# Running-sum copies of v's seven products on VectorE, new orders on every engine, and two small VectorE operations in another form

## The reference, cut to what matters

```python
x  = L0_attn_x                          # (16, 512, 256)
xn = layernorm(x)
q, k, v = xn @ wq, xn @ wk, xn @ wv     # 8 heads of 128
s  = rope(q) @ rope(k).T / 128          # causal mask, then softmax
attn = (softmax(s) @ v) @ wo
h  = relu(s0 * ([xn, -xn] @ sign(k0))) * 2
h  = relu(s1 * (h @ sign(k1))) * 2
ffn = s2 * (h @ sign(k2))
out = x + attn + ffn
```

## Time and profile before

| | |
|---|---|
| median of 3 runs | 1731.85 us |
| the profiled execution's own time | 1731.84 us |
| its span | 1730.0 us |
| TensorE matmuls busy | 1698.8 us, 98% |
| ScalarE busy | 1515.6 us, 88% |
| VectorE busy | 1429.8 us, 83% |
| GpSimd busy | 970.0 us, 56% |

### The profile page before, as it was taken

One profiled execution on the slowest core, in us unless ns is written; L12 is line 12 of the kernel. 1 busy time (PEld: TensorE's weight loads), 2 busy tenths in 40 slices (PEclk: granted clock), 3 DMA queues, 4 the chain that ended last, 5 costly groups with the idle time before them and its releaser, 6 DMA issues.

```text
span 1730.0 us, 35715 instructions
## 1 busy us (share of the span) xinstructions
PE 1698.8 (98%) x13340; PEld 1259.3 (73%) x13340; DVE 1429.8 (83%) x3440; ACT 1515.6 (88%) x3310; POOL 970.0 (56%) x775
## 2 busy tenths in 40 slices
PE   6999999999999999999999999999999999999998
PEld 3567767777777777777877777777777777777777
DVE  8997888787888888788787887878888887987875
ACT  6898898988989889898998989889898898989984
POOL 7764745557465474654656455474654746546441
PEclk9999999999999999999999999999999999999999
DMA  5243534434434454445344434344354445344343
GB/s 176 49 78 65 100 66 92 91 69 80 88 84 80 79 82 74 92 68 95 68 77 86 86 80 88 72 81 86 84 83 80 80 74 92 68 98 71 66 86 68
DMA packets 486046, 142.05 MB, mean 82 GB/s; under 512 B 465904, under 2 KB 484848, under 8 KB 485872
## 3 DMA queue, kind: packets, MB, share of 16 engines
q1 hardware_dynamic: 485872, 139.76, 42.6%
HBM read 14.94 MB, written 8.39 MB: 13 GB/s over the span
## 4 chain that ended last, share of the span: by engine, by line
PE 89%; DVE 3%; ACT 3%; DMA 3%; SPq 1%; issue 1%; POOL 0%; DVEq 0%
PE bank L276 33%; PE bank L806 21%; PE bank L774 11%; PE bank L757 11%; PE bank L795 8%; PE bank L817 5%; DMA pt<-ph 2%; DMA ph<-in_wv 1%; SPq L324 1%; DVE bank L663 1%; ACT ph L509 1%; ACT bank L505 1%; DVE ph L673 0%; DVE mx L670 0%; ACT tb L485 0%
## 5 line engine op out<-in xcount | busy, mean ns | idle before, releaser
L416 POOL TENSOR_TENSOR tb<-tb,sin 128x512 f32<-128x512 f32 x256 | 326.7, 1277 | 326.9 <-ACT tb L485 325.1
L419 POOL TENSOR_TENSOR qk<-tb,qk 128x512 f16<-128x512 f32 x256 | 298.1, 1167 | 286.2 <-ACT qk L488 285.5
L806 PE MATMUL bank<-hb,wa 128*128 128x256 f16 x3360 | 382.2, 273 | 0.0
L806 PEld LDWEIGHTS bank<-hb,wa 128*128 128x128 fp8e5 x3360 | 327.4, 98 | 43.3
L505 ACT ACTIVATE bank<-bank,nm,sc 128x512 f32<-128x512 f32 (+3 forms) x512 | 302.1, 590 | 3.4
L673 DVE SCALAR_TENSOR_TENSOR ph<-bank,mx,ph 128x512 f16<-128x512 f32 (+3 forms) x512 | 253.0, 543 | 16.3 <-ACT ph L509 15.7
L509 ACT ACTIVATE ph<-bank,mx 128x512 f16<-128x512 f32 (+3 forms) x512 | 232.5, 540 | 24.2 <-DVE mx L670 22.3
L663 DVE CUSTOM_DVE_ANT_0 bank<-bank,mask 128x512 f32<-128x512 f32 (+3 forms) x512 | 239.6, 512 | 13.0 <-PE bank L757 12.7
L774 PE MATMUL bank<-pt,v 128*128 128x256 f16 (+1 forms) x2304 | 232.5, 256 | 7.0 <-DMA pt<-ph 3.4
L757 PE MATMUL bank<-qk 128*128 128x512 f16 (+3 forms) x1536 | 230.0, 299 | 4.0 <-DVE tb L639 2.6
L774 PEld LDWEIGHTS bank<-pt,v 128*128 128x128 f16 x2304 | 203.5, 98 | 39.6 <-DMA pt<-ph 6.1
(11 more groups left out here) (138 smaller groups left out, 2617.4 us busy)
## 6 DMA issues: line engine op xcount, KB each, us to landing
out<-xnat SPq DMA_DIRECT2D x32, 256.0 KB, 2.1
xnat<-in_x SPq DMA_DIRECT2D x15, 512.0 KB, 3.9
pt<-ph SPq DMA_TRANSPOSE x256, 4.3
o<-in_k SPq DMA_DIRECT2D x1, 1024.0 KB, 8.3
v<-in_wq SPq DMA_DIRECT2D x1, 1024.0 KB, 10.4
v<-in_wk SPq DMA_DIRECT2D x1, 1024.0 KB, 12.0
ph<-in_wv SPq DMA_DIRECT2D x1, 1024.0 KB, 13.7
o<-in_wo SPq DMA_DIRECT2D x1, 1024.0 KB, 10.8
```

Source lines behind the costliest of these rows:

```text
L416: pool.tensor_tensor(tb, tb, SIN[:], ALU.mult).then_inc(s_crossed, 1)
L419: pool.tensor_tensor(QK[:, g % 2, 2 * w + 1, :], TB[:, (2 * g + w) % TRING, :], QK[:, g % 2, 2 * w, :], ALU.subtract).then_inc(s_qk_lo, 1)
L806: mm = pe.matmul(ps[:, 256 * u:256 * u + 256], WA[:, w, k, (2 * j + u) * 128:(2 * j + u) * 128 + 128], HB[:, h, s, k, :], start=first and ...
```

## The change

- The two copies of v's running sums per group are made by `copy_v` on VectorE and counted by a semaphore of their own, `s_vcopy`; the second layer's copies stay on ScalarE.
- The written orders of all five queues are laid anew, with other banks, other places of the loop's cut, and other waits; the set of operations is otherwise the same.
- The last instruction of `power_of_two` is split into two of one column each.
- The multiplication in `inverse` goes over its four columns in the order 0, 2, 1, 3, as a pattern of two by two with steps 1 and 2.

```diff
+        s_vcopy = sem("s_vcopy")
...
-            dve.tensor_scalar(DG[:, i:i + 2], ID[:, 0:2], AR[:, i + 1:i + 2], 2.0 ** -6,
+            dve.tensor_scalar(DG[:, i:i + 1], ID[:, 0:1], AR[:, i + 1:i + 2], 2.0 ** -6, ALU.mult, ALU.mult)
+            dve.tensor_scalar(DG[:, i + 1:i + 2], ID[:, 1:2], AR[:, i + 1:i + 2], 2.0 ** -6,
                               ALU.mult, ALU.mult).then_inc(s_pow, 1)
...
+        def every_other(v):
+            return v.rearrange("p (a b) -> p b a", a=2)
+
         def inverse(dve, g):
             dve.reciprocal(RI[:, g % 4, :], SM[:, g % 4, :]).then_inc(s_recip, 1)
             dve.wait_ge(s_recip, g + 1)
-            dve.tensor_scalar(RK[:, g % 4, :], RI[:, g % 4, :], 4096.0, None, ALU.mult).then_inc(s_inv, 1)
+            dve.tensor_scalar(every_other(RK[:, g % 4, :]), every_other(RI[:, g % 4, :]), 4096.0, None,
+                              ALU.mult).then_inc(s_inv, 1)
```

SyncE, batch 2 (the transposes of heads 21 and 22 change places; the loop has the same exchange in every batch):

```diff
-            sp.wait_ge(s_P_lo, 88)
+            sp.wait_ge(s_P_lo, 92)
             sp.wait_ge(s_PV, 20)
+            turn_p(sp, 22)
+            sp.wait_ge(s_PV, 21)
             turn_p(sp, 21)
-            sp.wait_ge(s_P_lo, 92)
-            sp.wait_ge(s_PV, 21)
-            turn_p(sp, 22)
```

The second group's copies of v in the loop, TensorE and VectorE after the change (these lines are all new):

```diff
+                scores(pe, 8 * b, 2, ps[4])
+                pe.wait_ge(s_P_lo, 32 * b - 3)
+                qk(pe, 8 * b + 1, 0, ps[2])
+                pe.wait_ge(s_P_lo, 32 * b - 1)
+                layer2(pe, 1, ps[6])
+                pe.wait_ge(s_P_lo, 32 * b)
+                v_product(pe, b, 1, 1, ps[0])
+                pe.wait_ge(s_o, 8 * b - 2)
+                qk(pe, 8 * b + 2, 0, ps[5])
+                pe.wait_ge(s_vcopy, 4 * b - 1)
+                v_product(pe, b, 1, 6, ps[0])
+                qk(pe, 8 * b + 3, 1, ps[2])
+                v_product(pe, b, 1, 2, ps[7])
+                pe.wait_ge(s_vcopy, 4 * b)
+                v_product(pe, b, 1, 7, ps[6])
...
+                add_ffn(dve, b - 1, 1, ps[6])
+                dve.wait_ge(s_vs, 14 * b - 6)
+                copy_v(dve, ps[0], ps[7])
+                dve.wait_ge(s_exp, 32 * b + 4)
+                inverse(dve, 8 * b)
+                dve.wait_ge(s_P_hi, 32 * b + 1)
+                p_lo(dve, 8 * b, 3, ps[3])
+                dve.wait_ge(s_vs, 14 * b - 5)
+                dve.wait_ge(s_ffn, 2 * b)
+                copy_v(dve, ps[0], ps[6])
```

More of the change, by code:

```diff
@@ new lines, in tensor_program @@
+            pe.wait_ge(s_vcopy, 4)
+            v_product(pe, 1, 1, 3, BANK[0])
+            pe.wait_ge(s_pt[1], 128)
+            pe.wait_ge(s_o, 7)
+            values(pe, 7, BANK[3])
+            v_product(pe, 1, 1, 7, BANK[4])
+            pe.wait_ge(s_rot, 21)
+            pe.wait_ge(s_WAa, 5)
+            product(pe, 0, 1, range(8), BANK[6], first=True)
+            pe.wait_ge(s_qk_lo, 18)
+            pe.wait_ge(s_rot, 22)
+            scores(pe, 8, 0, BANK[7])
+            pe.wait_ge(s_o, 8)
@@ new lines, in tensor_program @@
+            product(pe, 0, 5, range(8), BANK[3], first=True)
+            pe.wait_ge(s_P_lo, 37)
+            qk(pe, 13, 1, BANK[7])
+            pe.wait_ge(s_copy, 2)
+            product(pe, 0, 3, range(8), BANK[6])
+            v_product(pe, 1, 1, 4, BANK[4])
+            pe.wait_ge(s_pt[0], 160)
+            pe.wait_ge(s_P_lo, 39)
+            values(pe, 8, BANK[0])
+            pe.wait_ge(s_qk_lo, 22)
+            pe.wait_ge(s_P_lo, 40)
+            scores(pe, 10, 0, BANK[2])
+            pe.wait_ge(s_rot, 26)
@@ new lines, in tensor_program @@
+            product(pe, 1, 6, range(8), BANK[4])
+            pe.wait_ge(s_P_lo, 83)
+            product(pe, 1, 5, range(8), BANK[2], first=True)
+            pe.wait_ge(s_copy, 8)
+            product(pe, 1, 3, range(8), BANK[4])
+            product(pe, 1, 7, range(8), BANK[0])
+            pe.wait_ge(s_pt[0], 320)
+            pe.wait_ge(s_P_lo, 84)
+            values(pe, 18, BANK[5])
+            pe.wait_ge(s_qk_lo, 47)
+            pe.wait_ge(s_rot, 47)
+            scores(pe, 22, 0, BANK[3])
@@ new lines, in tensor_program @@
+            pe.wait_ge(s_h1, 14)
+            scores(pe, 22, 1, BANK[4])
+            pe.wait_ge(s_P_lo, 85)
+            scores(pe, 22, 2, BANK[6])
+            pe.wait_ge(s_P_lo, 87)
+            pe.wait_ge(s_xT, 48)
+            qk(pe, 24, 1, BANK[1])
+            pe.wait_ge(s_P_lo, 88)
+            qk(pe, 23, 0, BANK[7])
+            pe.wait_ge(s_h1, 15)
+            v_product(pe, 3, 0, 1, BANK[2])
+            product(pe, 1, 4, range(8), BANK[0])
+            pe.wait_ge(s_vcopy, 9)
+            pe.wait_ge(s_xTT, 48)
@@ L5987, in tensor_program @@
-            product(pe, 1, 2, range(8), BANK[3])
+            scores(pe, 27, 0, BANK[7])
+            pe.wait_ge(s_P_lo, 107)
+            scores(pe, 27, 1, BANK[0])
+            pe.wait_ge(s_P_lo, 108)
+            scores(pe, 27, 2, BANK[3])
+            pe.wait_ge(s_rot, 58)
+            product(pe, 0, 1, range(8), BANK[5], first=True)
+            pe.wait_ge(s_pt[0], 416)
+            pe.wait_ge(s_rot, 59)
+            values(pe, 24, BANK[4])
+            pe.wait_ge(s_copy, 9)
+            product(pe, 0, 2, range(8), BANK[6])
@@ L6003, in tensor_program @@
[L6003 to L6012 removed]
+            qk(pe, 30, 1, BANK[2])
+            pe.wait_ge(s_h1, 19)
+            scores(pe, 29, 0, BANK[0])
@@ new lines, in tensor_program @@
+                scores(pe, 8 * b + 3, 2, ps[2])
+                pe.wait_ge(s_rot, 16 * b + 10)
+                product(pe, 0, 1, range(8), ps[1], first=True)
+                pe.wait_ge(s_pt[0], 128 * b + 32)
+                pe.wait_ge(s_rot, 16 * b + 11)
+                values(pe, 8 * b, ps[6])
+                pe.wait_ge(s_copy, 4 * b - 3)
+                product(pe, 0, 2, range(8), ps[0])
+                product(pe, 0, 6, range(3), ps[1])
+                pe.wait_ge(s_h0t, 4 * b)
+                product(pe, 0, 6, range(3, 8), ps[1])
@@ new lines, in tensor_program @@
+                pe.wait_ge(s_rot, 16 * b + 13)
+                product(pe, 0, 5, range(8), ps[3], first=True)
+                pe.wait_ge(s_pt[1], 128 * b + 32)
+                pe.wait_ge(s_rot, 16 * b + 14)
+                values(pe, 8 * b + 1, ps[7])
+                pe.wait_ge(s_h1, 8 * b - 7)
+                product(pe, 1, 1, range(8), ps[0], first=True)
+                pe.wait_ge(s_qk_lo, 16 * b + 12)
+                pe.wait_ge(s_P_lo, 32 * b + 13)
+                scores(pe, 8 * b + 4, 0, ps[4])
```

6879 lines of the change are left out of this document (3391 added, 3488 removed), and 28 rows, old and new, of the table ROTATION.

## The result

| | before | after |
|---|---|---|
| median, first measurement (20 runs of each) | 1731.2 us | 1728.83 us (1725.82 to 1730.14) |
| ratio, first measurement | | 0.9984 [0.9977, 0.9990] |
| ratio, measured again beside the experiments | | 0.9975 [0.9965, 0.9985] |
| profiled execution: own time, span | 1731.84, 1730.0 us | 1725.82, 1724.0 us |

The change makes the kernel faster by 2.4 us in the first measurement and by 4.4 us in the second (1731.27 to 1726.84). The forecast was 8.3 us, 1723.5. The profiled execution of after was the fastest of its 20 and flatters the change by 3 us, while that of before lay at its median; so the 6.0 us between the two spans aren't to be taken for the gain.

The account below looks back on a forecast made before the run. TensorE's matmuls were taken to bound the kernel from 264 to 1580 us, leaving gains at the ends; -0.6 - 2.7 - 0.9 - 2.5 - 0.8 - 0.8 = -8.3 us from 1731.84 gave 1723.5 us, range 1716 to 1734.

Parts of the forecast that it names:

- What bounds the kernel: From 264 to 1580 us TensorE's matmuls bound, with 1.2 us at most to give; the rest lies at the two ends.
- The term of -0.8 for the middle: In the middle batches, longer distance from `scores` to `values` removes TensorE's few transpose waits: -0.8 of 1.2 us.
- The split, -0.6: Before the second layer, two one-column instructions shorten TensorE's wait for the power of two: net -0.6 us, bounds 0 and -1.2.
- The multiplication of `inverse`, -2.7 and -0.9: New pattern might escape GpSimd's holds: -2.7 us at 248 us, including the low clock, and -0.9 at 1643 us.
- Held as before: Rival: the new pattern changes nothing for the multiplication, so 2.7 and 0.9 do not come; 1727.1 us, chance 0.20.
- the one case seen is not this one: Argument against Held as before: the held strided case had adjacent output; no row showed an operation with both sides strided.
- The copies, "worth 0 in itself": Moving 60 copies to VectorE at 700 ns, +42 us of its work, makes neither engine the bound: worth 0.
- Slower: Rival: in each loop batch v_product 7 waits for VectorE's copy, 1.4 us x 11 = 15 us; 1738.9 us, chance 0.13.
- The orders, -2.5, -0.8 and -0.8: New orders reduce TensorE's waits: -2.5 us from 60 to 224 us, -0.8 in the middle, -0.8 at the end.
- The two full engines: Rival: ScalarE and VectorE keep the first 224 us's waits, new ones replacing those removed; 1728.5 to 1730 us, chance 0.18.
- The last term, head 127, -0.8: At the end, `add_ffn` moves behind head 127's chain, shortening TensorE's 1.01 us transpose wait: -0.8 us, bounds 0 and -1.0.

Follow-up runs that it names:

- a5_columns: Kernel after, with the multiplication of `inverse` as four one-column instructions for the two held heads per batch (g >= 20, g % 8 in (0, 5)): 1726.33 us, 0.9970 of before.
- b3_columns: Kernel before, with the multiplication of `inverse` as four one-column instructions for heads 15 and 121 only: 1727.84 us, 0.9978 of before.
- b1_split: Kernel before, with only the last instruction of `power_of_two` split into two of one column: 1729.73 us, 0.9988 of before.
- b4_split_columns: Kernel before, with the split of `power_of_two` and single-column multiplications for heads 15 and 121, no copy moved or order changed: 1725.61 us, 0.9970 of before.
- b2_three_one: Kernel before, with the multiplication of `inverse` as three columns and one for heads 15 and 121 only: 1731.13 us, 0.9996 of before.
- d1_copies: Kernel before, with only the 60 copies of v's running sums moved to VectorE, each where ScalarE's began: 1742.64 us, 1.0060 of before.

## Why the prediction was wrong

The forecast was a gain of 8.3 us; 2.4 and 4.4 came. By its steps:

**What bounds the kernel: right.** The middle had 1.2 us to give, and gave nothing: the mean batch of the loop is 105.07 us before and 105.09 after, against 104.92 of TensorE's work. Before lost 1.7 us in three batches; after loses 0.17 us in every one, in front of v_product 7 (`a5_columns`, where the multiplication isn't held, doesn't lose it). The term of -0.8 for the middle was paid back by that new wait.

**The split, -0.6: right in mechanism, small.** Two instructions of 0.20 and 0.21 us where one took 1.57; 1.5 us measured on the kernel before, of which a part may be the low clock at 254 us that its profile lacks, and 0.8 on the kernel after, within the noise.

**The multiplication of `inverse`, -2.7 and -0.9: the size was right, the cause wrong.** Freed of its hold at just these two places (`b3_columns`), the kernel before gains 3.5 us of the 3.6 forecast: 1.7 of waiting at 248 us (3.4 where the low clock comes with it) for the 2.7, and 1.6 at 1643 us for the 0.9, which was half of a hold of 1.8 that lay on the path almost whole. Charging the low clock to the hold was a guess: `b1_split` has the wait without it. But the new pattern frees nothing. In the kernel after the gain at 248 us comes because the head reaches its multiplication 1.2 us ahead of GpSimd's operation; that was luck of the new order, and nothing in the prediction foresaw it. The rival *Held as before* named this way out ("by luck of where GpSimd works") and gave it no price, which was the fault in it: with 0.20 of the chances it was the true case for the mechanism, and the larger part of the 3.6 us came all the same (the 16th to the 24th reciprocal take 3.3 us less, and the end from the 112th 1.1 less, of which the last head has a part). The Trainium skill (Vector Engine (DVE) Microarchitecture Reference, section 5.1) lets a copy, a cast or a `tensor_scalar` from SBUF to SBUF take both ports where the outermost dimension that isn't one is even, or where it is odd and the same on both sides. The prediction told the first half of that rule and left out the second, and the kinds of operation. If taking both ports is what makes an operation wait for GpSimd, the traces agree with both halves: two by two held, and three columns held for 0.87 to 2.08 us, but not the reciprocal, which is of another kind (at most 0.18 us). I should have followed it in the forecast, and not the thought that "the one case seen is not this one".

**The copies, "worth 0 in itself": the step that failed, with the term for the orders below.** The size of a copy was right (0.693 us for 0.70) and so was the load of both engines. But the working asked only whether an engine becomes full. With the old orders the copies cost 11 us with VectorE at 85%, since each engine works in order and the copy pushes what stands behind it. The rival *Slower* had the very mechanism and named the wrong victim: it counted the slack of v_product 7, 1.3 us at most, and it was `v_lo`, directly behind the copy in the list, that had no slack. The 1.1 us a batch from which it would decide was near the 0.87 measured for the copies without the orders. In the kernel after its victim is the right one, at 0.17 us a batch.

**The orders, -2.5, -0.8 and -0.8: the other half of the same fault.** They were costed as a gain on top. Alone, with the copies on ScalarE, they cost 5 us. With the copies they make room for 60 x 0.69 us on VectorE, and that is where their gain goes: a loss of 11 us and a loss of 5 by themselves, about nothing together. In 60 to 224 us TensorE's idle time went from 8.2 to 7.6 us, not to 5.7, and the time up to the 16th reciprocal lies in the same range with old and new orders (the first column of the table above). Net of both, copies and orders gave nothing beyond the escape at 248 us that the measurement can tell: `b4_split_columns`, without them, stands at 0.9970.

**The last term, head 127, -0.8: half of it.** `add_ffn` left the chain, and from the head's reciprocal to its `values` the kernel after takes 10.22 us where before took 11.05. TensorE's wait fell only from 1.01 us to 0.64; it wasn't tried by itself:

```profile
1714.61 1.82 PE L780 MATMUL bank<-pt,v 128*128 128x256 f16 x18 [0.64 <-DMA pt<-ph]
```

So of the sum, -4.2 was due to things that can be had with a few single-column instructions (the split and the hold), and about that much came (2.4 and 4.4 us; `b4_split_columns` with these alone, 5.3). The other -4.1 stood for the orders, and, but for about 0.4 us at the end, it was not there, since the zero beside it was not a zero. The rivals' times were the better ones: 1727.1 us of *Held as before* lies between the two measurements, and 1728.5 us, the lower end of *The two full engines*, by the first of them; the latter's reason, a new wait in the place of each one removed, is near to the true one.

## What to carry to other kernels

Ask of a moved instruction what stands directly behind it in its new engine's list and how much slack that has, not how full the engine is; where engines work in order, work in front of an operation without slack costs time at 85% load too (here 0.87 us in every batch, for four copies of 0.69). When a change moves work and lays new orders, cost the two as one term, and look whether one collision that the new order happens to miss carries the gain: here two held instructions, of 0.17 us of work each, carried 3.5 us. Take such a collision away where it is, in a form that isn't held, and don't count on the phase to miss it.

## What the runs showed of the hardware

- A `tensor_scalar` on VectorE from SBUF to SBUF, of two to four columns, is held until a GpSimd operation of two tensors that has begun ends, whatever its pattern: four adjacent columns, two by two, three, and two (0.87 to 2.08 us for the multiplications of the lines above). It ends 0.02 to 0.03 us behind GpSimd's. A single column isn't held: of the 108 in `a5_columns` 92 lie wholly inside such an operation, and the longest took 155 ns. Exceptions are few: a three-column one at about 6.5 us of every kernel took 0.20 us, and a multiplication that began within 0.003 us of GpSimd's (as at 217.46 us of `b2_three_one`) took 0.17.
- A reciprocal of the same size, also from SBUF to SBUF with one source, isn't held: 33 before and 54 after began while GpSimd worked, and none took over 180 ns. Beside GpSimd's own `tensor_scalar` (L384 of before) the multiplication took 0.27 us, once in every batch from 301 us on, and ended 0.65 us before it.
- It matters which begins first: in the earlier trace rows the multiplication began 0.08 us behind GpSimd's and took 2.08 us, while 13 in the kernel after that began up to 0.10 us ahead of a GpSimd operation, and overlapped it, took 0.17.
- A wait of TensorE can be followed by a low clock, and needn't be. Behind the 2.5 us wait for the same `p_lo` the granted clock fell to 0.51 for 3.5 us in before (from 254 us) and in `b2_three_one` (from 256 us), and stayed at 1.00 in `b1_split` and in `d1_copies`. In before the stage took 1.7 us longer than in `b1_split`. I can't say what makes the difference.
- At the start the granted clock varies between executions of one kernel: the kernel after was low from 15.0 us for 3.4 us in one profile, and from 9.0 us for about 10 in the next. In its 20 runs the time goes with the mean clock (0.997 in the fastest, 0.993 in the seven slowest). That isn't so for every kernel: of before's runs one with 0.997 took 1731.12 us, near its median, and `b1_split` had 0.996 in its fastest run and in its slowest.
